# Attention scores for the maxima: the bias added from its float16 part by four 64x64 products instead of two over 128 rows

## The reference

```python
scores = jnp.einsum('bhnqd,bhnkd->bhnqk', qw, kw) * scale + pos_bias[None, :, None]
probs = jax.nn.softmax(scores, axis=-1)
ow = jnp.einsum('bhnqk,bhnkd->bhnqd', probs, vw)
# overlapping windows are averaged, then
x = _layernorm(x + ctx @ Wo + bo)
logits = x @ router_w.T          # best two of 8 experts, sigmoid gates
h = silu(x @ w_gate[e]) * (x @ w_up[e])
x = _layernorm(x + sum over the two of gate * (h @ w_down[e]))
```

## Time and profile before

| | |
|---|---|
| median of 3 runs | 740.96 us (737.52 to 741.58) |
| profiled execution | 740.13 us |
| its span, first to last instruction | 738.4 us |
| TensorE busy | 637.5 us, 86% |
| VectorE, ScalarE, GpSimd busy | 70%, 50%, 58% |
| attention (to about 489 us), experts (to about 692), final norm | three parts of the span |

### The profile page before, as it was taken

One profiled execution on the slowest core, in us unless ns is written; L12 is line 12 of the kernel. 1 busy time (PEld: TensorE's weight loads), 2 busy tenths in 40 slices (PEclk: granted clock), 3 DMA queues, 4 the chain that ended last, 5 costly groups with the idle time before them and its releaser, 6 DMA issues.

```text
span 738.4 us, 33034 instructions
## 1 busy us (share of the span) xinstructions
PE 637.5 (86%) x13242; PEld 493.3 (67%) x13242; DVE 514.3 (70%) x1624; ACT 371.0 (50%) x546; POOL 431.5 (58%) x482
## 2 busy tenths in 40 slices
PE   3779999999999999999999999889999999995000
PEld 1346667666667666666666666679999999995000
DVE  6835776776787687777777767857886776664185
ACT  2133444444444544544444434467677777773076
POOL 7720435645546546646546555577777777777454
PEclk9989999999999999999999999999999999999555
DMA  6895337436355455465374451134335443331494
GB/s 160 243 272 148 120 95 190 135 103 187 111 136 157 129 156 149 122 169 148 103 190 130 111 173 33 29 101 139 102 111 159 110 106 111 104 99 51 158 404 153
DMA packets 83575, 103.53 MB, mean 140 GB/s; under 512 B 15488, under 2 KB 70144, under 8 KB 83424
## 3 DMA queue, kind: packets, MB, share of 16 engines
q1 hardware_dynamic: 71040, 73.87, 35.8%
q0 software_dynamic: 8640, 17.84, 7.6%
q10 hardware_dynamic: 3744, 9.70, 3.5%
HBM read 60.12 MB, written 40.79 MB: 137 GB/s over the span
## 4 chain that ended last, share of the span: by engine, by line
PE 64%; DVE 9%; DMA 7%; issue 6%; SPq 6%; POOL 4%; ACT 2%; ACTq 1%; DVEq 0%; POOLq 0%
PE o_ps L1339 5%; PE score_ps L1293 5%; PE o_ps L1463 4%; PE ctx_ps L1463 4%; PE ctx_ps L1353 4%; PE scoret_ps L1299 4%; SPq L278 4%; PE scoret_ps L1316 3%; PE o_ps L1333 3%; PE score_ps L1283 3%; DMA blocks<-scratch 3%; PE bank L1210 3%; DMA scratch<-qk_hl 2%; PE scoret_ps L1283 2%; PE score_ps L1450 2%
## 5 line engine op out<-in xcount | busy, mean ns | idle before, releaser
L295 POOL DMA_INDIRECT slots<-rows_sb,slot_at x128 | 127.5, 996 | 132.1 <-PE o_ps L1339 84.5
L831 DVE TENSOR_REDUCE neg_max<-score_ps 128x16 f32<-128x1024 f32 x109 | 133.3, 1223 | 84.6 <-PE score_ps L1283 83.0
L710 ACT ACTIVATE prob<-scoret_ps 128x1024 f32<-128x1024 f32 x109 | 111.6, 1024 | 133.2 <-PE scoret_ps L1283 130.4
L560 POOL DMA_INDIRECT results<-scaled_sb,result_at x142 | 136.4, 961 | 43.1 <-issue 35.2
L743 ACT CAST w_slot<-wgu_sb 128x1024 fp32r x71 | 74.6, 1051 | 0.2
L1339 PE MATMUL o_ps<-v_sb,prob 128*64 128x18 f32 x2048 | 70.1, 210 | 2.8 <-issue 2.8
L1293 PE MATMUL score_ps<-bias_hl,fold 128*128 128x512 f16 x218 | 66.8, 389 | 3.2 <-DVE neg_max L831 3.2
L1339 PEld LDWEIGHTS o_ps<-v_sb,prob 128*64 128x64 f32 x2048 | 66.4, 138 | 3.5 <-issue 3.3
L1299 PE MATMUL scoret_ps<-bias_hl,fold 128*128 128x512 f16 x218 | 66.1, 385 | 0.2 <-ACT prob L710 0.2
L689 ACT COPY v_sb<-bank 64x512 f32<-64x512 f32 (+1 forms) x64 | 36.0, 563 | 52.4 <-PE bank L1271 31.9
L1353 PE MATMUL ctx_ps<-diag,o_sb 128*64 128x64 f32 x896 | 52.2, 234 | 10.2 <-DVE o_sb L846 5.0
(11 more groups left out here) (186 smaller groups left out, 1528.8 us busy)
## 6 DMA issues: line engine op xcount, KB each, us to landing
stack<-scratch SPq DMA_DIRECT2D x32, 512.0 KB
blocks<-scratch SPq DMA_DIRECT2D x126, 128.0 KB
scratch<-qk_hl SPq DMA_DIRECT2D x120, 128.0 KB
xin<-slots SPq DMA_DIRECT2D x71, 130.0 KB, 2.3
blocks<-results ACTq DMA_DIRECT2D x16, 512.0 KB, 10.1
x_sb<-in_x SPq DMA_DIRECT2D x16, 256.0 KB
out<-y_sb SPq DMA_DIRECT2D x16, 256.0 KB, 3.0
results<-scaled_sb,result_at POOLq DMA_INDIRECT x142
```

The source lines that it names most:

```text
L295: nc.gpsimd.indirect_dma_start(slots, bass.IndirectOffsetOnAxis(ap=slot_at[:, k % 2, n:n + 1], axis=0), rows_sb[:, k % 2, n // TT, n % TT, ...
L560: pool.indirect_dma_start(results, bass.IndirectOffsetOnAxis(ap=result_at[s % RBUF][:, t:t + 1], axis=0), scaled_sb[:, s % RBUF, t, :], No ...
L710: act.activation(prob[:, (par + u) % 2, :], turned_scores(i, u)[:, :, :].rearrange("p b c -> p (b c)"), ACT.Exp).then_inc(exp_done, 1)
L831: dve.tensor_reduce(neg_max[:, par, :, v, :], ps[:, :, :].rearrange("p b (h k) -> p b h k", k=W), AX_X, ALU.max, negate=True).then_inc(max ...
```

## The change

`bias_s` uses the float16 part of the bias alone. `bias_hl` then holds for the plain bias the float16 part in both halves of its rows, and the subtraction on VectorE goes over the turned bias alone. For the scores for the maxima the rest of the bias, below float16, is left out; the turned scores, from which the exponential is taken, have both parts as before. In place of two products on the whole 128x128 array there are four on 64x64 tiles: rows 64n to 64n + 63 give bank n, columns 64a to 64a + 63 the half a of the partitions.

```diff
@@ VectorE, start
-                dve.tensor_tensor(bias_hl[64:128, :, :], prob[64:128, :, :], bias_hl[64:128, :, :],
+                dve.tensor_tensor(bias_hl[64:128, 1, :], prob[64:128, 1, :], bias_hl[64:128, 1, :],
                                   ALU.subtract).then_inc(dve_made, 1)
@@ TensorE, bias_s
                     after(pe, max_done, NU * k + v - behind)
-                    for n in range(2):
-                        pe.matmul(ps[:, n, :], fold[:, :], bias_hl[:, 0, n * 512:n * 512 + 512],
-                                  start=True, stop=False, skip_group_check=True)
+                    for a in range(2):
+                        for n in range(2):
+                            pe.matmul(ps[64 * a:64 * a + 64, n, :], fold[64 * n:64 * n + 64, 64 * a:64 * a + 64],
+                                      bias_hl[64 * n:64 * n + 64, 0, n * 512:n * 512 + 512],
+                                      start=True, stop=False, skip_group_check=True)
```

## The result

The changed kernel took 740.73 us in the median of 20 runs (730.05 to 755.11), the kernel before 740.94 (737.52 to 751.04) on the same chip. The ratio of the two is 0.9931, with a 95% interval of 0.9902 to 0.996, when runs over 1.5% above the fastest of their kernel are left out as slow, and that takes out 9 of the 20 after but 1 of the 20 before. So on this chip 0.7%, or some 5 us, rests on that choice: the two medians of all runs differ by 0.2 us only. The changed kernel's times scatter more. The profiled execution took 736.86 us, its span is 735.1.

The account below looks back on a forecast made before the run. TensorE was taken to bound the attention, nearly balanced by a transfer chain. Savings of 6.4 + 3.6 + 1.7 + 1.1 + 1.3 = 14.1 us off the profiled 740.13 gave 726.0 us, range 718 to 734.

Parts of the forecast that it names:

- The cost of a call: Each `bias_s` on TensorE: 0.20 us less behind `bias_t` (77 calls), 0.29 less for unit 1 (14 calls).
- unit 0: `bias_s` for unit 0 of the step after next: 0.45 becomes 0.34 us, saving 0.10 in each of 14 calls.
- Rivals 3 and 4: Four products run as two successive pairs: 3, weight loads hidden, 739, chance 0.07; 4, a load exposed, 746, chance 0.05.
- The two added products and two added weight loads per call ... cost nothing of their own: TensorE in `bias_s`: 448 more instructions beside 26,484 add no time.
- Nothing else ends last there: Steps 1 to 13 outside the transfer chain: savings of units 1 and 2 arrive whole, 6.4 us.
- The transfers' part: Steps 1 to 13 inside the transfer chain: 3.6 us kept of 9; the rest becomes waits of `scores` for `blocks`.
- The waits for the maxima and for `exp` do not grow: TensorE's waits for the maxima and `exp` stay, since nothing is removed between a unit's scores and the next `bias_s`.
- the step at `turn_maxima`: Steps 1 to 13: unit 6's saving of 0.20 us mostly goes into `turn_maxima`'s wait for VectorE's last maximum.
- step 0's 1.7: Step 0 has much slack in its transfers, so its calls' savings arrive: 1.7 us.
- The start: Before the attention: half the VectorE subtraction gives 0.6 us, closer maxima of step 0 give 0.7, together 1.3.
- rival 2: Attention: the transfers keep all that is inside them and start no earlier, 730, or 733 if they stretch; chance 0.20.
- Rival 1: Attention: all of TensorE's saving arrives, 718 us; needs transfers to get shorter with the step; chance 0.17.

Follow-up runs that it names:

- e11: Changed kernel with `bias_s` as two products on 64x128 tiles in place of four on 64x64; ratio to the kernel before 0.9955.
- e1: Kernel before with each product of `bias_s` cut into two of 256 columns, 448 more instructions as in the changed kernel; ratio to the kernel before 0.9995.
- e17: Changed kernel, meant to add 64 instructions that do nothing; the built program has none, so the changed kernel again; ratio to the kernel before 0.9942.
- e18: Changed kernel, meant to shift instructions by 128 that do nothing; the built program has none, so the changed kernel again; ratio to the kernel before 0.9928.
- e14: Changed kernel with half the bytes in the loads of `stack` and `blocks` for the turned scores alone; ratio to the kernel before 0.995.
- e16: Changed kernel with the loads of `blocks` for the turned scores spread, some held back to later turns; ratio to the kernel before 0.9914.
- e7: Changed kernel with half the bytes in the stores and in all loads of `stack` and `blocks` from step 2 on; 722.7 us, ratio to the kernel before 0.9729.
- e6: Kernel before with half the bytes in the stores and in all loads of `stack` and `blocks` from step 2 on; 735.6 us, ratio to the kernel before 0.9890.
- e12: e9 with VectorE's choice of experts (`top_two`, `gates`) a turn later, behind the last maximum; ratio to the kernel before 0.9981.
- e10: Changed kernel with three more `bias_s`, results overwritten, ahead of `scores` for unit 0 in turn 7; ratio to the kernel before 0.9997.
- e9: Changed kernel with `scores` for unit 0 of the step after next behind `context` and `values` of turn 7, not ahead; ratio to the kernel before 0.9925.
- e15: Changed kernel with half the bytes in the loads of `stack` and `blocks` for the maxima's scores alone; ratio to the kernel before 0.9957.

## Why the prediction was off

The sign was right, the size was not: 14 us forecast, 3.3 in the profiled execution and 4 to 5 in the runs.

- **The cost of a call** was right for 91 of the calls: 0.20 and 0.29 less. For unit 0 the term was mis-sized: `bias_s` to V is 0.34 as forecast, but V's first group now takes 0.64 to its second, before 0.54, so that of the 14 x 0.10 nothing is left. The step's sum came out all the same, 1.39 less in least distances as forecast, because the product with the maxima behind `bias_s` takes 0.22 in place of 0.24; that is luck. The four products run side by side as L1316's did, in 0.24. Rivals 3 and 4 fall. The Trainium skill (TensorE: Matmul & The Clock Gate, Part 3, The mechanism) says that a weight load overlaps with products in flight only where its row group differs. Taken strictly that would put the pairs in one row group one after the other, and the 0.24 does not show it. The change of tile costs 0.10, as forecast; e11 adds a second instance of 0.08.
- **"The two added products and two added weight loads per call ... cost nothing of their own"**: true for their number (e1) but not for their place. Instructions arrive in blocks of 256, the blocks come late behind bursts of transfers, and the change gave a step 28 more instructions, 5.90 blocks in place of 5.79, so that a boundary stays longer in the stretch where it hurts, and made the engine faster than its instructions there: issue grew from 6.5 to 13.1 us. This is the largest missing term. How much of it comes of the 28 instructions and how much of the faster step no run separates: e1, with 1510 a step at the old pace, had 8 stalls of 2.5 us at the boundaries, and the changed kernel on a chip of that kind 9 and 11 of 4.9 and 5.6 (e17, e18). I had the stalls in the trace of before, 0.98 and 0.71 us among them, and put no term for them.
- **"Nothing else ends last there"** (outside the chain of transfers) is the step that failed with it. Of the 6.4 us it was to bring, the stalls behind the turned loads took 3.7 (0.2 before); with those loads halved or spread (e14, e16, e7) there are none.
- **The transfers' part**, 3.6 us kept and 5.5 turned into waits, was right in size: waits of transfers grew by 4.6. But the distance from `stack` to the scores is not 7.0 everywhere: it is 6.4 to 8.4, mean 7.3, and only six of 13 steps wait, some for 1.3 to 2 us.
- **"The waits for the maxima and for `exp` do not grow"**: those for VectorE grew by 4.4, of which the step at `turn_maxima` was to take 2.6. VectorE's share is the same work in a shorter step, and the change took away from the time between the last maximum and its readers.
- **The clock** was not in the sum. Behind longer waits it falls to 1.2 GHz, two stretches of 1.3 us each, the start (0.50 for 0.84 in 30 to 40 us: 1.6 us of step 0's 1.7), and the first 5 us of the experts, which with what follows lose 3.3 us.
- **The start** brought 1.8, not 1.3.
- **The rivals**: nearest is rival 2, 730 to 733, in which the transfers keep all that is inside them; the measured 736 lies beyond it, as none of the rivals had the stalls. Rival 3's number, 739, is as near, but its mechanism (0.44 a call) is not what the trace shows. A step takes 28.2 on average (28.4 before) and not 27.6 to 28.0. Rival 1 (718) is what comes near when the transfers are halved (e7 against e6: 12.9 us).

How far the growth of the maxima's waits is a consequence of the stalls, each execution deciding anew, is not settled; e12, made for it, moved the waits and lost time at the end of the attention. The clock's share is read from the profile and not shown by a run of its own.

## What to carry to other kernels

Where TensorE bounds a stretch and is fed by transfers that are nearly as long, shortening its products turns into waits, and halving the bytes is worth more than moving the loads: here 5 us became 13 (in runs that leave half of q and k old, so that they show what the bytes cost and are no kernel to use). Before a change is costed at its products' price, list the stalls named issue, number them through the program, and see whether they lie a block apart and behind bursts of transfers; they are a resource like another, and the remedy for one wait (a later load, an order that gives more time) can feed them. Two kernels with the same products can differ by where a block of instructions ends in the loop.

## What the runs showed of the hardware

- TensorE's instructions come in packets of 16 KB, 256 instructions of 64 bytes, counted over loads, products, waits and register instructions together. Where a packet is late, the engine stops at number 193 to 195 of the 256, for 0.2 to 2.4 us, and goes on 1.2 to 1.6 us after the packet's end (19 stalls after, 24 in e10). In the kernel before, the changed one, e9 and e10 nearly all of the stalls named issue are of this kind (74 of 80); on the chips with the longer experts a third (e17 9 of 30, e18 11 of 30).
- These packets wait behind the transfers of the kernel: of those due in the 8 us behind L1210 none came late, of those due in the next 8, with the stores and the first loads, a third to three quarters did (before, after, e9, e10). Halving or spreading the loads of the turned scores ends the stalls behind them (e7, e14, e16: 0 of 44; e15, without it: 5 of 15).
- Behind waits of 0.62, 0.26 and 1.25 us (after, 232 to 237 us) the granted clock was at 1.2 GHz from 239 to 242 us, and in e9 behind a late block of 2.24 us it was 0.50 in 188 to 191.
- Four products on 64x64 tiles over both row halves and both column halves take 0.24 us for 512 columns, in either order of the loop.
- The kernel before took 741 to 743 us on three chips and 834 to 841 on three others, the ratio of two kernels being alike.
